# Cross-attention and gated FFN in one kernel: value products over two pairs of PSUM banks, output accumulators alternating from tile 1, last product and store in halves, new instruction orders

## What is computed

```python
# x: (4, 256, 256), ctx: (4, 256, 128), both f32; residuals around both parts
q = ctx @ Wq.T + bq;  k = ctx @ Wk.T + bk
att = softmax(q @ k.T)                       # (4, 256, 256)
x = x + layernorm(x) @ att.T                 # "x_m[l,m] = sum_n x[l,n] att[m,n]"

def bit_linear(x, w, b):
    sx = 127 / max(|x| over the row, 1e-5);  xq = clip(round(x * sx), -128, 127) / sx
    gw = mean(|w|);                          wq = clip(round(w / gw), -1, 1) * gw
    return xq @ wq.T + b

h = layernorm(x)                             # 1024 rows of 256
p = silu(bit_linear(h, gate_w, gate_b)) * bit_linear(h, val_w, val_b)   # hidden size 1024
x = x + bit_linear(p, out_w, out_b)
```

## Time and profile before

| | |
|---|---|
| median of 3 runs | 60.62 us (60.6 to 60.66) |
| the profiled execution | 61.23 us, of it a span of 59.5 us |
| busy, share of the span | PE 86%, DVE 81%, ACT 80%, POOL 76% |
| granted PE clock | full in all 40 slices |
| loads from HBM | 6.04 MB, nearly all in the first 19 us |
| first exponential, first SiLU, last SiLU start at | 10.35, 28.14, 48.99 us |
| last DVE residual ends at | 57.31 us |

### The profile page before, as it was taken

The page is one execution under the profiler, slowest core; times in us unless marked ns, Lnnn a source line. Parts: engine busy times, 40 slices in busy tenths (PEclk is TensorE's granted clock), DMA queues, the critical chain, the costliest instruction groups (busy, mean ns, idle before and its releaser), DMA issues.

```text
span 59.5 us, 1140 instructions
## 1 busy us (share of the span) xinstructions
PE 51.0 (86%) x298; PEld 32.6 (55%) x301; DVE 48.3 (81%) x122; ACT 47.6 (80%) x84; POOL 45.0 (76%) x102
## 2 busy tenths in 40 slices
PE   1999993999999699929899988899999998889910
PEld 1768842958888478713323634333473753669800
DVE  3249858887999899997998989898999997997150
ACT  0723927999999999978999684999999999698700
POOL 4970006199789888798879978989999999999900
PEclk9999999999999999999999999999999999999999
DMA  0687989999995000000002000399170199920573
GB/s 0 167 305 285 339 315 392 408 406 414 398 409 219 4 6 11 0 6 0 6 0 44 0 0 15 73 174 178 40 147 0 23 184 180 237 81 0 176 232 121
DMA packets 11069, 8.92 MB, mean 150 GB/s; under 512 B 7604, under 2 KB 9140, under 8 KB 11064
## 3 DMA queue, kind: packets, MB, share of 16 engines
q1 hardware_dynamic: 10912, 8.72, 47.4%
q10 hardware_dynamic: 152, 0.14, 0.9%
HBM read 6.04 MB, written 1.05 MB: 119 GB/s over the span
## 4 chain that ended last, share of the span: by engine, by line
POOL 30%; PE 30%; issue 19%; DVE 10%; ACT 5%; POOLq 0%; ACTq 0%
POOL h L344 6%; PE psG L763 5%; PE psO L940 5%; PE psT L778 5%; PE psT L753 5%; POOL r_cols L276 4%; PE psV L763 4%; PE psH L940 3%; POOL rstd L311 3%; ACT o_early L723 3%; DVE x L485 3%; POOL pgam L325 2%; DVE nmax L467 2%; POOL res L372 2%; POOL w_int L409 2%
## 5 line engine op out<-in xcount | busy, mean ns | idle before, releaser
L572 DVE TENSOR_REDUCE pmax<-prod 128x1 f32<-128x1024 f32 x8 | 9.7, 1210 | 0.1
L707 ACT ACTIVATE sil<-psG,s_gv 128x1024 f32<-128x1024 f32 x8 | 8.9, 1111 | 0.6 <-PE psG L874 0.2
L556 DVE TENSOR_TENSOR prod<-psV,sil 128x1024 f32<-128x1024 f32 x7 | 8.5, 1221 | 0.9 <-ACT sil L707 0.5
L859 PE MATMUL psG<-ter_gate,hT 128*128 128x512 bf16 x31 | 8.0, 378 | 0.8 <-ACT sil L707 0.7
L886 PE MATMUL psV<-ter_val,hT 128*128 128x512 bf16 x26 | 7.0, 382 | 0.2 <-issue 0.2
L940 PE MATMUL psO<-ter_out,pT 128*128 128x256 bf16 x48 | 6.2, 272 | 0.7 <-ACT o_early L723 0.7
L940 PEld LDWEIGHTS psO<-ter_out,pT 128*128 128x128 bf16 x48 | 4.4, 98 | 2.4 <-DVE pT L599 0.8
L694 ACT ACTIVATE hT<-psH,unshift 128x256 bf16<-128x256 f16 x8 | 3.8, 474 | 1.5 <-PE psH L842 1.4
L859 PEld LDWEIGHTS psG<-ter_gate,hT 128*128 128x128 bf16 x32 | 2.7, 96 | 4.0 <-issue 2.0
L664 ACT ACTIVATE p_int<-prod,pqs 128x1024 int16<-128x1024 f32 x4 | 4.6, 1141 | 0.0
L715 ACT CAST pT<-pT_int 128x1024 bf16<-128x1024 int16 x4 | 4.2, 1038 | 0.5 <-DMA pT_int<-p_int 0.5
(11 more groups left out here) (142 smaller groups left out, 145.3 us busy)
## 6 DMA issues: line engine op xcount, KB each, us to landing
w_gate<-in_w_gate SPq DMA_DIRECT2D x2, 512.0 KB, 5.5
x<-in_x_tok SPq DMA_DIRECT2D x4, 256.0 KB, 7.1
w_val<-in_w_val SPq DMA_DIRECT2D x2, 512.0 KB, 7.3
xt_sb<-in_x_T SPq DMA_DIRECT2D x4, 256.0 KB, 7.9
w_out<-in_w_out SPq DMA_DIRECT2D x2, 512.0 KB, 8.9
out_x<-res SPq DMA_DIRECT2D x8, 128.0 KB, 1.8
ctx_sb<-in_ctx_T SPq DMA_DIRECT2D x2, 128.0 KB, 2.8
ctx_sb<-in_ctx_T SPq DMA_DIRECT2D x1, 256.0 KB, 6.8
```

The source lines that it names most:

```text
L556: nc.vector.tensor_tensor(prod[:, t % P_RING, :], psV[:], sil[:, t % S_RING, :], ALU.mult).then_inc(prod_done, 1)
L572: nc.vector.tensor_reduce(pmax[:, t:t + 1], prod[:, t % P_RING, :], AX.X, ALU.max, apply_absolute_value=True).then_inc(pmax_done, 1)
L707: nc.scalar.activation(sil[:, t % S_RING, :], psG[:], ACT.Silu, scale=s_gv[:, t, 0:1]).then_inc(sil_done, 1)
L859: nc.tensor.matmul(psG[:, c * HC:(c + 1) * HC], hT[:, t, k, :], w_ter[0][:, k * HID + c * HC:k * HID + (c + 1) * HC], start=(k == 0), stop ...
```

## The change

It keeps every arithmetic step and moves many. In words:

1. **PSUM**: psT becomes an f32 tensor of two banks. Value products of even tiles go to psV, of odd tiles to psT (`ps_v`), so that the value half of biases(t) waits for the product of tile t-2 instead of t-1. The PE transposes of p for tiles 6 and 7 go into psG and a half of psV, after the last SiLU.
2. **ALT = 1**: output products alternate between psO and psH from tile 1 on.
3. **Last tile**: last_product(7) is computed in two column halves of 128 (16 matmuls instead of 8), into psH and psV, with a residual and a store for each half (64 KB each).
4. **apply_att(b)** is split into its two tiles, so that h_transpose(0) stands between the two of batch 3.
5. **Work changes engines**: q_out(1) to ACT, k_out(2) to DVE; normalise(2) from DVE to ACT; centre_x2(2), (4) to ACT and (3) stays there; to_int(0,1) to POOL, to_int(2,1) to ACT; scales_h(1), (2) to POOL; h_step(1) to DVE; all gamma_p to POOL; p_round_int: ACT keeps 0 and 1 of its 1, 2, 4, 5, POOL has 2, 3, 4 instead of 0 and 3, DVE has 5; p_round(6) from POOL to DVE; widen: ACT 0 to 4, DVE 5; p_copy_half from ACT to DVE; p_round_half changes sides.
6. **Warm-up**: 24 matmuls of 128 columns instead of 12 of 256.
7. **New orders** in all five lists.

```diff
-    WARM = 12
+    WARM = 24
...
-        ALT = 5
+        ALT = 1
         ps_o = [psH[:, 0:D] if t >= ALT and t % 2 else psO[:, 0:D] for t in range(T)]
+        ps_last = [psH[:, 0:P], psV[:, HC:HC + P]]
...
+        ps_v = [(psV, psT)[t % 2] for t in range(T)]
+        ps_p, ps_p_last = psG[:, 0:HC].bitcast(F16), [psG[:, HC:HID].bitcast(F16), psV[:, 0:HC].bitcast(F16)]
...
+            def store_half(c):
+                sp.wait_ge(late_done, LAST - LATE + 1 + c)
+                sp.dma_start(out_t[:, LAST, c * P:(c + 1) * P], res[:, LAST, c * P:(c + 1) * P]).then_inc(stored, 16)
...
+            def p_round_int(t):
+
+                dve.wait_ge(pqs_done, t + 1)
+                if t >= I_RING:
+                    dve.wait_ge(turned[t % I_RING], 16 * (t // I_RING))
+                nc.vector.tensor_scalar(p_int[:, t % I_RING, :], prod[:, t % P_RING, :], pqs[:, t:t + 1], None,
+                                        ALU.mult).then_inc(pround_done[t], 1)
...
+            def add_residual_half(c):
+
+                dve.wait_ge(o_done, T + c)
+                dve.wait_ge(zb_done, T)
+                dve.wait_ge(so_done, T)
+                half = slice(c * P, (c + 1) * P)
+                nc.vector.scalar_tensor_tensor(res[:, LAST, half], ps_last[c], s_o[:, LAST:T],
+                                               res[:, LAST, half], ALU.mult, ALU.add).then_inc(late_done, 1)
...
+                    elif g == 2 and t == 1:
+                        pe.wait_ge(x2_done, 3 * TB)
                     elif g == 2:
-                        pe.wait_ge(prod_done, t)
-                    mm = nc.tensor.matmul((psG, psV)[g // 2][:, g % 2 * HC:(g % 2 + 1) * HC],
+                        pe.wait_ge(prod_done, t - 1)
+                    mm = nc.tensor.matmul((psG, ps_v[t])[g // 2][:, g % 2 * HC:(g % 2 + 1) * HC],
...
+                for i in range(2):
+                    pe.wait_ge(pT_sb_half[i], 1)
+                    for c in range(2):
+                        for k in range(i * KH // 2, (i + 1) * KH // 2):
+                            mm = nc.tensor.matmul(ps_last[c], pT[:, t % T_RING, k * P:(k + 1) * P],
+                                                  w_ter[2][:, k * D + c * P:k * D + (c + 1) * P], start=(k == 0),
+                                                  stop=(k == KH - 1))
+                        if i:
+                            mm.then_inc(o_done, 1)
```

245 lines of the change are left out of this document (124 added, 121 removed).

## The result

| | before | after |
|---|---|---|
| median (range, executions) | 60.64 us (60.60 to 60.99, 4) | 62.59 us (62.20 to 62.91, 4) |
| ratio to before, 95% interval | | 1.031 (1.024 to 1.038) |
| the profiled execution, its span | 61.23, 59.5 | 62.61, 60.6 |
| first exponential, first SiLU, last SiLU start at | 10.35, 28.14, 48.99 | 8.56, 26.49, 47.06 |
| last_product(5) starts at | 53.56 | 54.22 |

The prediction was 59.3 us and faster; the kernel is slower.

The account below looks back on a forecast made before the run. No engine alone bounds it; the chain changes hands. Start -1.65, loop -0.65, tail giving back 0.65: -1.65; store issue makes it -1.5, interference costs 0.2; 60.62 - 1.3 = 59.3 us, range 58.5 to 60.6.

Parts of the forecast that it names:

- Start: Up to the first SiLU: reordered loads and redistributed work bring it from 28.14 to 26.5, a gain of 1.65 us.
- Loop: First to last SiLU: ACT's work between SiLUs thinned, 20.2 us against 20.85, a gain of 0.65.
- worth little: Loop, psV and psT alternating: removes a cycle of 2.7 us but leaves the psG cycle of 2.64.
- Tail: Last SiLU to last residual: ends at 55.65 against 57.31, giving back 0.65 of the 2.3 us won before.
- For interference ... 0.2: DVE's longer SBUF passes slowing POOL: 0.2 us set against the gain.
- Rival (b): Tail: DVE passes shut POOL out, gamma_p(7) about 0.3 late, or dearer product pairs; 59.6 to 59.7, both 60.0; chance 0.08.
- Rival (c): POOL's rounding late: p_int(4) expected at 45.6, kernel slower from 47.6 on, 61.0 us at 48.0; chance 0.14.
- The warning on add_bias_shift(7): Tail, POOL's last work: done at 54.9, only 0.3 ahead; forecast wrong if a last residual waits for it.
- DVE's rounding of 1024 columns: Tail, on DVE: taken as 0.85 us, at most 1.0 at double rate or 1.22 at the reduction's.
- The product in halves: Last product on PE: 16 pairs at 56 ns, 0.90 us against 0.87; second residual half starts during the first.
- Store: Store in halves: SP's last issue starts about 55.75, 0.1 us late; smaller pieces given nothing, at best 0.2.

Follow-up runs that it names:

- exps_first: tile5_on_pe with stores 3 and 4 on ACT, whole last product, widen(3) later, exps(0) before abs_sum(0,0), invert_sum(0) before k_out(2); 61.38 us, ratio 1.010.
- tail_reordered_whole: Changed kernel with old warm-up, gamma_p(5) to (7) on DVE, tiles 5 and 6 rounded on ACT, tail lists reordered, last product whole; 61.74 us, ratio 1.015.
- gamma_dve: Changed kernel with gamma_p(5) and gamma_p(7) made by DVE instead of POOL; 62.98 us, ratio 1.011.
- both_dve: Changed kernel with gamma_p(5), gamma_p(7) and add_bias_shift(7) moved from POOL to DVE; 62.82 us, no ratio given.
- tile5_on_pe: Changed kernel with old warm-up, tail work moved between engines, and tile 5 rounded on ACT and transposed by PE without DMA; 62.01 us, ratio 1.014.

## Why the prediction was wrong, point by point

- **Start: right.** First exponential at 8.56 (8.9 was taken, 8.6 to 9.3 the bounds), w_gate's late half waited for 0.41 (0.2), first SiLU at 26.49 (26.5). The reason is not shown: exps_first has the exponentials' own start off the path. The warm-up, which the sum gave no value, is no large part: the changed kernel and its variants have their first SiLU at 25.85 to 26.70 with the new one (seven profiles) and at 26.29 to 26.94 with the old one (six, without exps_first and the profile of tail_reordered_whole, whose clock was 0.973). In the kernel before it is 27.64 against 28.14, one profile each.
- **Loop: half the gain, and wrong in reason.** 20.57 us against 20.2, so 0.28 gained instead of 0.65, last SiLU 47.06 against 46.7. The first step took 3.02 instead of 2.7, the third 3.00 instead of 2.85. The alternation was called "worth little"; in this order it is worth 1.56.
- **Tail: the step that failed.** The sum has DVE never wait for POOL's gammas: halves at 48.0, and "p_round(6) ... runs while POOL makes gamma_p(7)"; then "from its end PE sets the pace", with last_product(5) at 51.85. It came at 54.22, 2.37 late, in two parts. DVE waited 0.98 for gamma_p(5), so the halves began at 49.64 and p_round(6) ended at 52.83 instead of 51.4: 1.43. And last_product(5) needs tile 5 widened, which DVE does behind the reciprocal of tile 7. POOL made gamma_p(7) only at 53.34, DVE waited 0.83 for it, and last_product(5) came 1.39 behind p_round(6) instead of 0.45: 0.94. From there 3.50 to the end against 3.8 by the sum, plus the wait of 0.72 for add_bias_shift(7): 58.44 against 55.65. gamma_dve bears out the first two waits: with both gammas on DVE last_product(5) comes 6.35 behind the last SiLU's start instead of 7.16.
- **The transpose of tile 5** has no date in the sum either. By the sum's own dates it would have been in time (rounded by 48.0, turned by 51.1, widened by 51.5). As it ran, the rounding ended at 49.72 and the integers were turned at 52.8, so without the second wait last_product(5) would by an estimate (52.8 plus 0.43 for the widening) still have come after 53.2.
- **"For interference ... 0.2": too small.** s_o took 586 ns in the mean against 398 before. The three waits for POOL are 2.53 us in the profile, and removing them gave 1.06 (both_dve, with 1.02 more work on DVE). How much of them is interference and how much POOL's order is not shown.
- **Rival (b)** let gamma_p(7) come about 0.3 behind p_round(6), with POOL locked out. DVE waited 0.83. POOL was at work without a gap: three residual additions, 2.09 us from 50.09, then two scales, 1.19 us where two took 0.65 in the kernel before. By these rows about 0.5 is an estimate of the lock-out, and the list ahead of the gamma is the rest.
- **Rival (c)** had p_int(4) at 45.6 and slower from 47.6 on. It was done at 47.46, the mechanism nearly there: POOL did not start 1.65 earlier but 0.7 (inverse_parts(1) at 28.17, before 28.86), and last_product(4) waited 0.86 for widen(4). But p_transpose(6) behind it waited for DVE's p_round(6), which ended 0.2 later still; in gamma_dve, where DVE is earlier, the wait for widen(4) (1.03) does hold PE up. The dearer effect of the late rounding was gamma_p(5) right behind it on POOL, which no rival priced. The warning on add_bias_shift(7) (done at 54.9, 0.3 ahead) came true: done at 57.74, 0.72 late.
- **DVE's rounding of 1024 columns:** 0.75, taken as 0.85. **The product in halves:** four pairs start every 0.22 to 0.23 us, 56 ns a pair as the transposes, not the 81 that the Trainium skill (TensorE: Matmul & The Clock Gate, Back-to-back issue gap) gives for a sustained stream; inside the span halves cost and gave nothing.
- **Store:** issued as the last residual ends, as forecast in kind; its queue binds only once the tail is shorter (tile5_on_pe).

## To carry to other kernels

In a sum over a tail, give a date to every input of each step on the path, the small ones and the transfers too: here two scales of one column (0.28 and 0.29 us) on POOL had none, and DVE waited 1.81 us for them. Compare the end to several candidate starts over all profiles. The one that it follows at a constant distance (here last_product(5), at 3.7 us, or 4.2 with a last wait for POOL, while the last SiLU was 8.3 to 11.9 ahead) is where the last stall ends in most of these kernels. What it waits for can differ from kernel to kernel, and is read from the waits. The work that feeds it goes ahead of work that doesn't, even of the stage that looked like the pacemaker: in the kernel before, one exchange that broke this cost 1.34 us. And moving work off a busy engine helps only if it is not ahead of the path on the next: with two roundings on ACT tile 7 came nearer to its SiLU by 0.8 us and the end by nothing.
